# Line rows of the attention stage: other tables in memory, other loads, another place in the queue

## What is computed

```python
w1 = (x_prev @ w1_write.T).reshape(B, T, H, pd);  w2 = (x @ w2_write.T).reshape(B, T, H, pd)
write_lines = exterior(w1, w2)          # 6 numbers a token and head, of length 1
read_lines = exterior(r1, r2)
J_write = jnp.einsum('bthi,ij->bthj', write_lines, _J6)
incidence = jnp.einsum('bqhp,bkhp->bhqk', read_lines, J_write)
weights = decays[:, None, None] ** diffs_pos[None] * past[None].astype(x.dtype)
logits = std_logits + incidence * weights[None] * bias_scale[None, :, None, None]
attn = softmax(where(causal_mask, -inf, logits));  out = attn @ v
```

## Time and profile before

| | us |
|---|---|
| time, median of 3 runs | 1222.98 (1220.91 to 1224.81) |
| profiled execution, its own time | 1230.04 |
| its span from the first to the last instruction | 1228.3 |
| mean granted clock of TensorE in it | 0.921 |
| busy: PE, PEld | 989.3, 768.3 |
| busy: DVE, ACT, POOL | 773.1, 722.4, 810.2 |

### The profile page before, as it was taken

The page is one execution under the profiler, slowest core; times in us unless marked ns, Lnnn a source line. Parts: engine busy times, 40 slices in busy tenths (PEclk is TensorE's granted clock), DMA queues, the critical chain, the costliest instruction groups (busy, mean ns, idle before and its releaser), DMA issues. The chain is left out here.

```text
span 1228.3 us, 31465 instructions
## 1 busy us (share of the span) xinstructions
PE 989.3 (81%) x9473; PEld 768.3 (63%) x9473; DVE 773.1 (63%) x2061; ACT 722.4 (59%) x1612; POOL 810.2 (66%) x1351
## 2 busy tenths in 40 slices
PE   2457888888888888788888888888797199999967
PEld 2336666666666666666666666666575188888853
DVE  6565566666666767666666776666674556555545
ACT  3435666666666767666766776667656155555530
POOL 6455567777767777776777777777734446666654
PEclk9998889898988989988999999999988589999988
DMA  7444445455445455545454555545451144333339
GB/s 206 126 140 145 145 128 155 144 153 146 142 136 149 140 151 149 153 135 153 130 153 142 148 152 151 161 131 155 133 146 48 41 109 144 91 92 91 85 102 361
DMA packets 229731, 170.78 MB, mean 139 GB/s; under 512 B 65536, under 2 KB 191808, under 8 KB 229440
## 3 DMA queue, kind: packets, MB, share of 16 engines
q1 hardware_dynamic: 214736, 143.23, 40.8%
q0 software_dynamic: 8448, 17.45, 4.4%
q10 hardware_dynamic: 6384, 8.09, 1.9%
HBM read 90.81 MB, written 77.07 MB: 137 GB/s over the span
## 5 line engine op out<-in xcount | busy, mean ns | idle before, releaser
L926 DVE TENSOR_REDUCE peak<-pre 128x6 f32<-128x768 f32 x256 | 244.5, 955 | 148.9 <-PE pre L766 146.0
L957 DVE TENSOR_TENSOR sc<-sc,decay 128x512 f32<-128x512 f32 x256 | 179.3, 700 | 129.0 <-PE sc L736 124.8
L1157 ACT ACTIVATE PT<-sc 128x768 f32<-128x768 f32 x256 | 205.0, 801 | 40.2 <-PE sc L753 37.4
L1643 POOL DMA_INDIRECT yab<-y_out,xt x136 | 131.5, 967 | 83.6 <-issue 63.4
L736 PE MATMUL sc<-QI,KI 100*128 100x128 bf16 x1024 | 103.7, 225 | 96.0 <-DMA QI<-kq_rows 95.6
L1365 POOL DMA_INDIRECT xg<-stage,slot_i x128 | 131.0, 1023 | 62.8 <-issue 38.5
L766 PE MATMUL pre<-causal,identb 128*128 128x256 bf16 x512 | 150.0, 293 | 0.0
L765 PE MATMUL pre<-KT,queries 84*128 84x256 bf16 x512 | 148.8, 291 | 0.0
L736 PEld LDWEIGHTS sc<-QI,KI 100*128 100x128 bf16 x1024 | 68.6, 100 | 105.8 <-DMA QI<-kq_rows 105.4
L764 PE MATMUL pre<-KT,queries 84*128 84x128 bf16 x512 | 119.3, 233 | 11.6 <-DVE peak L926 7.3
L1298 POOL TENSOR_TENSOR dim_part<-dim_rest,dim_part 128x512 bf16<-128x512 f32 x32 | 37.0, 1158 | 122.4 <-ACT dim_part L1213 122.4
(11 more groups left out here) (276 smaller groups left out, 2899.9 us busy)
## 6 DMA issues: line engine op xcount, KB each, us to landing
KT<-kq_rows SPq DMA_DIRECT2D x128, 168.0 KB
queries<-kq_rows SPq DMA_DIRECT2D x128, 168.0 KB
kq_rows<-dim_part SPq DMA_DIRECT2D x64, 192.0 KB, 2.0
kq_rows<-line_part SPq DMA_DIRECT2D x64, 144.0 KB
KI<-kq_rows SPq DMA_DIRECT2D x128, 72.0 KB
QI<-kq_rows SPq DMA_DIRECT2D x128, 72.0 KB
xt<-xg SPq DMA_DIRECT2D x136, 65.0 KB, 1.9
kq_rows<-dim_part SPq DMA_DIRECT2D x64, 128.0 KB, 1.9
```

The source lines that it names most:

```text
L926: nc.vector.reduce_max(peak[half][:, i:i + 2, 0:3], pre[:, :, 0:3 * P].rearrange("p n (g k) -> p n g k", g=3), AX.X)\
L957: nc.vector.tensor_tensor(seeded(p), seeded(p), decay[:, 2 * p:2 * p + 2, :].unsqueeze(2).broadcast_to([P, 2, NT, P]), ALU.mult).then_inc( ...
L1157: nc.scalar.activation(PT[p % 4][:], sc[:, window], ACT.Exp).then_inc(exped.sem, 1)
L1643: nc.gpsimd.indirect_dma_start(yab, bass.IndirectOffsetOnAxis(xt[r][:, D:D + 1].bitcast(i32), 0), y_out[r % 8][:], None).then_inc(y_sent[r ...
```

## The change

The table kq_rows is taken apart. dim_rows holds the 48 rows of dims. line_rows holds for each line row and head the 256 raw values and behind them the 128 decayed values that are not zero, so one store writes both (line_part is laid out in the same way, and the two instructions that fill line_val write to other places in it). The zeros are no longer in memory: the tiles KT and QF are set to zero where the decayed rows have none, once, in the setup, and the loads write the other half of each row. Loads go by halves of the heads (8) in place of quarters (4), and TensorE waits by halves. The peaks and the ones move from rows 84 to 86 to rows 96 to 98, with zeros in rows 84 to 95, so the scores read 99 rows.

SyncE's list per batch is now: load_peaks(b, 1), load_rows(b+1, 1), load_lines(b+1, 0), store_lines(b+2), load_peaks(b+1, 0), load_lines(b+1, 1), load_rows(b+2, 0), store_dims(b+3).

```diff
-NV = NM + NR
-DEC0 = NS * DH
-RAW0 = NS * NM
-TOP = NS * NV
+DIMS = NS * DH
+LINES = NS * NR
+PEAK0 = 96
+TOP = PEAK0 + 3
 MR = P // 2
-INC = MR + NS * NR
+INC = MR + LINES
+LW = T + P
...
-        kq_rows = [nc.dram_tensor(f"kq_rows{n}", (2, TOP, H, T), bf16).ap() for n in range(3)]
+        dim_rows = [nc.dram_tensor(f"dim_rows{n}", (2, DIMS, H, T), bf16).ap() for n in range(3)]
+        line_rows = [nc.dram_tensor(f"line_rows{n}", (2, LINES, H, LW), bf16).ap() for n in range(3)]
...
-                nc.gpsimd.memset(zero_rows[:], 0.0).then_inc(zeros_ok, 1)
...
-                    step(nc.gpsimd.memset(v["KT"][m][64:96].rearrange("p h t -> p (h t)").bitcast(u32), ones_pair))
+                    step(nc.gpsimd.memset(v["KT"][m][64:96].rearrange("p h t -> p (h t)").bitcast(u32), 0))
+                    step(nc.gpsimd.memset(v["KT"][m][96:P].rearrange("p h t -> p (h t)").bitcast(u32), ones_pair))
...
-                act.wait_ge(zeros_ok, 1)
-                for third in range(3):
-                    for kq, half in ((0, 1), (1, 0)):
-                        decayed = v["kq_rows"][third][kq, DEC0:RAW0].rearrange("(s r) h t -> (r h) s t", s=NS)
-                        act.dma_start(decayed[:, :, half * P:half * P + P],
-                                      zero_rows[0:6 * H].unsqueeze(1).broadcast_to([6 * H, NS, P])).then_inc(v["zeros_stored"], 16)
...
-                act.wait_ge(v["zeros_stored"], 16 * 6)
...
+                for m in range(2):
+                    nc.vector.memset(v["KT"][m][32:64].rearrange("p h t -> p (h t)").bitcast(u32), 0)
+                    nc.vector.memset(v["QF"][m][32:64].rearrange("p h t -> p (h t)").bitcast(u32), 0)
+                    nc.vector.memset(v["QF"][m][64:96].rearrange("p h t -> p (h t)").bitcast(u32), 0)
                 dve.wait_ge(ld_d, 16)
...
                     for kq in range(2):
-                        half = slice(kq * P, kq * P + P)
-                        spread(slots(jb, kq, "raw"), line_part[:, :, kq * T:(kq + 1) * T], kq, lines_stored.sem)
-                        spread(slots(jb, kq, "decayed")[:, :, half], line_part[:, :, 2 * T + kq * P:2 * T + (kq + 1) * P], kq, lines_stored.sem)
+                        spread(slots(line_rows[jb % 3][kq]), line_part[:, :, kq * LW:(kq + 1) * LW], kq, lines_stored.sem)
...
-                    for quarter in (2 * half, 2 * half + 1):
-                        heads = slice(4 * quarter, 4 * quarter + 4)
-                        done = rows_loaded[quarter].sem
-                        sp.dma_start(KT[par][0:RAW0, heads, :], kq_rows[jb % 3][0, 0:RAW0, heads, :]).then_inc(done, 16)
-                        sp.dma_start(QF[par][0:RAW0, heads, :], kq_rows[jb % 3][1, 0:RAW0, heads, :]).then_inc(done, 16)
+                    heads, done = slice(8 * half, 8 * half + 8), rows_loaded[half].sem
+                    for kq, tile in ((0, KT[par]), (1, QF[par])):
+                        sp.dma_start(tile[0:DIMS, heads, :], dim_rows[jb % 3][kq, :, heads, :]).then_inc(done, 16)
+                        sp.dma_start(tile[DIMS:DIMS + LINES, heads, kq * P:kq * P + P],
+                                     line_rows[jb % 3][kq, :, heads, T:LW]).then_inc(done, 16)
...
-                    for quarter in (2 * half, 2 * half + 1):
-                        heads = slice(4 * quarter, 4 * quarter + 4)
-                        done = lines_loaded[quarter].sem
-                        sp.dma_start(KI[MR:INC, heads, :], kq_rows[jb % 3][0, RAW0:TOP, heads, :]).then_inc(done, 16)
-                        sp.dma_start(QI[MR:INC, heads, :], kq_rows[jb % 3][1, RAW0:TOP, heads, :]).then_inc(done, 16)
+                    heads, done = slice(8 * half, 8 * half + 8), lines_loaded[half].sem
+                    for kq, tile in ((0, KI), (1, QI)):
+                        sp.dma_start(tile[MR:INC, heads, :], line_rows[jb % 3][kq, :, heads, 0:T]).then_inc(done, 16)
...
                 def body(b, par):
                     if live(b):
-                        load_lines(b, 1)
                         load_peaks(b, par, 1)
                     if live(b + 1):
                         load_rows(b + 1, 1 - par, 1)
+                        load_lines(b + 1, 0)
                     if live(b + 2):
                         store_lines(b + 2)
                     if live(b + 1):
-                        load_lines(b + 1, 0)
                         load_peaks(b + 1, 1 - par, 0)
+                        load_lines(b + 1, 1)
                     if live(b + 2):
                         load_rows(b + 2, par, 0)
...
-                    if p % 2 == 0:
-                        wait(pe, lines_loaded[p // 2], b)
+                    if p % 4 == 0:
+                        wait(pe, lines_loaded[p // 4], b)
...
-                        nc.scalar.activation(line_val[:, 0:2 * T], B[0:6 * H, :], ACT.Copy).then_inc(done, 1)
+                        nc.scalar.activation(line_val[:].rearrange("p (n k) -> p n k", n=2)[:, :, 0:T],
+                                             B[0:6 * H, :].rearrange("p (n k) -> p n k", n=2), ACT.Copy).then_inc(done, 1)
...
```

More of the change, by code:

```diff
@@ L18 @@
 E, HF = 8, 256
-NS, NM, NR = 6, 14, 6
+NS, NR = 6, 6
 COMP_K = ((0, 3, 0), (3, 2, 1), (5, 1, 2))
@@ L169, in build @@
         ident = sb(whole, "ident", [P, P])
[L170 removed]
+        mod_stored, w_loaded = sem("mod_stored"), sem("w_loaded")
         attention = whole.enter_context(ExitStack())
@@ L637, in hold, with slots @@
                     settle(sp, sp_settled)
-                def slots(jb, kq, rows):
-                    first, last = {"dims": (0, DEC0), "decayed": (DEC0, RAW0), "raw": (RAW0, TOP)}[rows]
-                    return kq_rows[jb % 3][kq, first:last].rearrange("(s r) h t -> (r h) s t", s=NS)
+                def slots(rows):
+                    return rows.rearrange("(s r) h t -> (r h) s t", s=NS)
                 def spread(dst, parts, kq, done):
@@ L749, in scores @@
                         first, second = slice(0, P), slice(P, T)
-                        nc.tensor.matmul(seeded(p)[:, n, 0, :], KT[par][0:top, h, first], QF[par][0:top, h, first], start=False, stop=True,
+                        nc.tensor.matmul(seeded(p)[:, n, 0, :], KT[par][0:TOP, h, first], QF[par][0:TOP, h, first], start=False, stop=True,
                                          skip_group_check=True)
-                        nc.tensor.matmul(across(p)[:, n, :], KT[par][0:top, h, first], QF[par][0:top, h, second], start=True, stop=True)
-                        last = nc.tensor.matmul(seeded(p)[:, n, 1, :], KT[par][0:top, h, second], QF[par][0:top, h, second],
+                        nc.tensor.matmul(across(p)[:, n, :], KT[par][0:TOP, h, first], QF[par][0:TOP, h, second], start=True, stop=True)
+                        last = nc.tensor.matmul(seeded(p)[:, n, 1, :], KT[par][0:TOP, h, second], QF[par][0:TOP, h, second],
                                                 start=False, stop=True, skip_group_check=True)
@@ L757, in prescores @@
                 def prescores(b, par, p):
-                    if p % 2 == 0:
-                        wait(pe, rows_loaded[p // 2], b)
+                    if p % 4 == 0:
+                        wait(pe, rows_loaded[p // 4], b)
                     wait(pe, maxed, b, p)
@@ L763, in prescores @@
                         h = 2 * p + n
-                        nc.tensor.matmul(pre[:, n, 0:P], QF[par][0:RAW0, h, 0:P], KT[par][0:RAW0, h, 0:P], start=True, stop=False)
-                        nc.tensor.matmul(pre[:, n, P:3 * P], QF[par][0:RAW0, h, P:T], KT[par][0:RAW0, h, :], start=False, stop=False)
+                        nc.tensor.matmul(pre[:, n, 0:P], QF[par][0:DIMS + LINES, h, 0:P], KT[par][0:DIMS + LINES, h, 0:P], start=True, stop=False)
+                        nc.tensor.matmul(pre[:, n, P:3 * P], QF[par][0:DIMS + LINES, h, P:T], KT[par][0:DIMS + LINES, h, :], start=False, stop=False)
                         last = nc.tensor.matmul(diagonal(pre, n), identb[:], causal[:].unsqueeze(1).broadcast_to([P, 2, P]),
```

34 lines of the change are left out of this document (16 added, 18 removed).

## The result

| | before | after |
|---|---|---|
| time, median, us | 1223.89 (1220.91 to 1229.57, 4 runs) | 1109.82 (1105.58 to 1112.36, 4 runs) |
| ratio, 95% interval | | 0.9059 [0.9013, 0.9106] |
| profiled execution, its span | 1230.04, 1228.3 | 1111.9, 1110.2 |
| mean granted clock | 0.921 | 0.955 |

The forecast was 1118 us between 1090 and 1160; the change makes the kernel 9.4% faster. The engines stand in the order PE, PEld, DVE, ACT, POOL, then the granted clock, the DMA share and GB/s.

A forecast was written before the change was run, and what follows sets the result against it. With the line-row wait gone, GpSimd was taken to bind at 23.6 us a batch: 1230.04 - 95 (26 steady batches) - 14 (early batches) - 7 (after them) + 4 (setup) = 1118 us, range 1090 to 1160.

The forecast's parts named there:

- The wait goes wholly: Steady attention: TensorE's wait for line rows before the incidences, 3.3 us a batch, should go with loads ahead of stores.
- The clock goes up with it: Steady attention: without the long wait, TensorE's granted clock rises from 0.92 to near 1.00.
- GpSimd is the bound: Steady attention: GpSimd's 23.4 us plus 0.2 handing over, 23.6 a batch, saves 95 us; range 23.3 to 24.0, chance 0.62.
- TensorE would need 22.7: Steady attention: a full-clock batch of 25.4 us less its wait of 2.69 leaves 22.7 for TensorE alone.
- TensorE stays the bound: Rival, steady attention: GpSimd's pauses shrink, a batch takes 22.7 us and the kernel 1095; chance 0.10.
- the clock stays down: Rival, steady attention: TensorE's 1 us wait brings the lower clock; batch 24.25 to 25 us, kernel 1135 to 1155; chance 0.14.
- Early batches -14, batch behind -7: Attention's ends: three batches before the steady part lose 14 us in waits and clock, the 27.0 us after it lose 7.
- none of L764 for the rows: Sign expected in the profile after: no TensorE wait for row loads before the prescores at L764.
- the 2.5 us to spare: Row loads land 2.0 us after issue, at 772.5; prescores want them 8.3 us after the incidences, at 775.0.
- Setup +4: Setup: added zero memsets on VectorE and GpSimd lengthen it by 4 us, bounds 0 and +8.
- By bytes 12.5 remain: DMA engines, steady attention: 13.6 us busy a batch falls to 12.5, as bytes fall from 3.55 to 3.26 MB.
- The rival made of that rule: Small row-load pieces land 6.7 us after issue: 1192 us, still faster, chance 0.08; at 8.3 us, 1255, slower, chance 0.03.

The follow-up runs named there:

- e1: The kernel before with only SyncE's order of issue from the change, keeping old tables, twelve line stores and loads by quarters: 1113.8 us, ratio 0.9139.
- e2: The changed kernel with its new tables but SyncE's old order, line rows behind the line stores: 1162.9 us, ratio 0.9538.
- e5: The changed kernel with only the first half of the line rows put back behind the six line stores: 1122.8 us, ratio 0.9215.
- e6: The changed kernel with the last split of the line rows moved from GpSimd to VectorE: 1086.1 us, ratio 0.8913.
- e12: The changed kernel with e8's setup and the last line and dimension splits moved to VectorE, the latter behind the next batch's first decay multiplication: 1091.1 us, ratio 0.8933.
- e3: The changed kernel with one more GpSimd subtraction a batch, into a tile that nobody reads: 1157.5 us, ratio 0.9513.
- e4: The changed kernel with the first prescore matmul of each head issued twice, sixteen more matmuls a batch: 1107.8 us, ratio 0.9076.
- e7: The changed kernel with the row loads of batch b+2 issued right behind the line stores, in front of the peaks: 1175.6 us, ratio 0.9647.
- e11: The changed kernel with e6's line split, e8's memsets, and row loads ahead of the second line half, behind the peaks: 1084.2 us, ratio 0.8838.
- e8: The changed kernel with six zero memsets moved from VectorE's setup to its idle time in the fill, GpSimd's two dropped: 1106.5 us, ratio 0.9085.

## Why the prediction was right, and where its sizes were off

*The wait goes wholly: right.* L730 waits 0.0 us, and e1 shows that the place in the queue is enough. That the loads stood behind the stores was the right reading; e2 and e5 add what the prediction had only touched, that the second half, behind the dimension stores, is the larger part once there are six stores. No run has the old place of the second half alone, so its part is e2's time less e5's.

*The clock goes up with it: right in the steady part, 0.92 to 0.99.* In the early batches it did not, as said below.

*GpSimd is the bound: right, its price 0.6 us a batch too high, and 0.3 under the case's own range.* The failing term is "all else ... 23.4 us a batch. Nothing in the change makes that shorter", and the 0.2 for handing over. That 23.4 counted every pause but one as fixed, and it is not "nearly all work": 524.41 / 26 = 20.2 of it is. One of them was a wait for VectorE's maxima, which wait for TensorE's prescores; its group before, 168 to 876.3 us:

```profile
L1331 POOL CAST peak_part<-peak 128x16 bf16<-128x16 f32 x52 | 10.8, 208 | 11.0 <-DVE peak L931 10.6
```

It falls to 2.1 us, 0.34 a batch; GpSimd's busy time falls by (524.41 - 521.15) / 26 = 0.13; 23.37 - 0.47 = 22.90, and 22.92 is measured in undisturbed batches. No handing over is needed. With 23.02 for the mean of 26, the term is 110 us and not 95; this is the whole error of the sum and more. Of the 15 us, 9 were paid back by the early batches and the batch behind, taken too high, and the rest of the span, left out; that 1118 lies so near 1110 is in part luck.

*TensorE would need 22.7: too high.* e6 and e12 show 22.1. The number was a batch less its one large wait and still held 25.4 - 21.20 - 2.69 = 1.5 us of short waits, of which e6 has (574.40 - 541.86) / 26 = 1.25 left; TensorE's busy time is also 0.36 a batch lower (20.84 against 21.20), and why is open. The rival "TensorE stays the bound" is out, by e3 and e4. The rival "the clock stays down" did not decide, but its mechanism is there: a little in the change, and over nine batches on end in e3.

*Early batches -14, batch behind -7: too much, -10.4 and -3.6.* Here two steps failed. One is "none of L764 for the rows": nearly true of the steady part (1.1 us in all), not of its ends. The last row load and the prescores that it holds, behind the steady part:

```profile
762.87 0.38 SPq L675 DMA_DIRECT2D queries<-line_rows  x1
```
```profile
767.43 0.23 PE L757 MATMUL pre<-KT,queries 84*128 84x128 bf16 x1 [2.11 <-DMA queries<-line_rows]
790.73 0.23 PE L757 MATMUL pre<-KT,queries 84*128 84x128 bf16 x1 [2.40 <-DMA queries<-line_rows]
```

Both halves of the 2.5 us to spare were off. The rows are there 767.43 - 763.25 = 4.2 us after their issue, and 3.2 one batch on (787.56 to 790.73), where the dimension stores' 2.0 were taken. And TensorE, in batches without the full set of jobs, wants them earlier: 767.43 - 2.11 is 6.3 us behind the batch's first incidences at 759.05, where 8.3 were read from a full batch. These waits are 3.8 us in the early batches and 12.6 over the run. The last of them lies in the rest, which the sum had left alone and which grew by 2.7. What it would take to end them is open: e7 and e11 moved the rows forward and did not end them.

The other step is the clock, of which the early batches were to get most of 0.10 back: it stayed at 0.91, from 0.90. TensorE's idle time fell by 6.9 us there (14.3 to 7.4), its busy time only by 3.5. In e8 the same batches run at 1.00 and come to 63.00, 13.6 less than before, near the 14 that were taken.

*Setup +4: right, +3.1.* VectorE's six memsets took until 14.03 us, short of the 14.89 up to which L408 was held before (beside GpSimd's cast into QI, from 11.27 to 14.86, as the trace has it, and not beside a memset). The chain did move with GpSimd's end, as predicted: GpSimd's last memset ends at 24.56 in place of 21.04, VectorE's chain at 30.81 in place of 27.30, 3.5 us each.

```profile
24.40 0.16 POOL L320 MEMSET VP<- 128x32 f32 x1
```

How much VectorE's own six would have cost alone wasn't parted, since e8 moved both. "VectorE: DVE Perf Modes", section on zero memsets issued as uint32, of the Trainium skill gave an estimate of 12.8 us for six; the trace has 14.03 - 1.28 = 12.75 from first start to the next instruction, but as 1.76 busy and 0.38 to 0.46 of pause for each.

*Small pieces: no price in time, but the size was wrong.* "By bytes 12.5 remain" of DMA engine time a batch (the 3.55 and 3.26 MB behind it are 3.64 and 3.34 in the MB of the lines below, in the same proportion). Measured: 0.61 x 598.4 / 26 = 14.0 us, against 0.50 x 708.3 / 26 = 13.6 before and 0.60 x 605.2 / 26 = 14.0 in e1, which still moves the larger pieces. The bytes fall, as predicted (steady parts of e1 and after):

```profile
DMA packets 142822, 103.42 MB, mean 171 GB/s; under 512 B 44992, under 2 KB 116128, under 8 KB 142720
```
```profile
DMA packets 148678, 95.58 MB, mean 160 GB/s; under 512 B 40876, under 2 KB 141964, under 8 KB 148581
```

7.6% fewer bytes in 4% more packets take as much engine time as in e1. The rule of "DMA: Bandwidth & Descriptors", section Specifications, of the Trainium skill on transfers under 512 bytes doesn't explain it: these lines hold fewer packets under 512 bytes (40876 in place of 44992), and what grew are those from 512 bytes to 2 KB (101088 in place of 71136). Why the time did not fall with the bytes is open. The rival made of that rule did not come, since hardly a steady wait stands before L757. The wider scores (99 partitions) cost nothing: a score matmul takes 0.22 us, as it did.

## What to carry to other kernels

A DMA queue is an instruction stream: read for each load what is issued ahead of it, what that waits for, and who needs it first, then order by need; moving one load forward puts the next one behind its hold and its issue. An engine's floor is its period less all waits for others, the small ones too; the largest wait alone leaves the estimate high. Before moving work to an engine's idle time, check in which slot of its program that time stands and when its input is there, and try a bound from both sides: work added to one engine, work taken from it.

## What the runs showed of the hardware

With sixteen more matmuls a batch the profiled run had a granted clock of 1.00 over the whole steady part, where that of the change shows four stretches at the lower level (1.2 GHz); TensorE stood idle for (596.60 - 561.79) / 26 = 1.34 us a batch with them and for (598.40 - 546.52) / 26 = 2.00 without. One profile each doesn't show that the matmuls did it: over whole executions the clock is 0.952 to 0.974 in the four runs with them and 0.955 to 0.972 in the four without. Idle time by itself doesn't say which level is granted, though: the ten batches of e3 at 1.00 have (239.40 - 207.96) / 10 = 3.14 us of it each.

VectorE's independent memsets, with nothing to wait for, followed each other with 0.38 to 0.46 us between them, a fifth to a quarter of the 1.76 us that each takes.
